# A cross-attention layer and a recurrent layer on one core: the second batch's projections between the first batch's head groups, and nine GpSimd sums a round on VectorE

## The reference

```
scores = einsum('bhqd,bhkd->bhqk', q, k) / sqrt(32)
scores = scores * mask - 10000.0 * (1.0 - mask)
ctx = einsum('bhqk,bhkd->bhqd', softmax(scores), v)
```

```
a = k_t[:, None] * v_t[None, :]
out = einsum('i,ij->j', r_t, u * a + s)
s = a + w_t[:, None] * s
```

## Time and profile before

| | us |
|---|---|
| median of 3 runs (2052.15 to 2056.28) | 2054.96 |
| the profiled execution | 2053.13 |
| its span, first to last instruction | 2051.4 |
| TensorE busy | 1899.5 (93%) |
| VectorE busy | 1445.3 (70%) |
| ScalarE busy | 870.5 (42%) |
| GpSimd busy | 486.0 (24%) |

### The profile page before, as it was taken

One profiled execution on the slowest core, in us unless ns is written; L12 is line 12 of the kernel. 1 busy time (PEld: TensorE's weight loads), 2 busy tenths in 40 slices (PEclk: granted clock), 3 DMA queues, 4 the chain that ended last, 5 costly groups with the idle time before them and its releaser, 6 DMA issues.

```text
span 2051.4 us, 29340 instructions
## 1 busy us (share of the span) xinstructions
PE 1899.5 (93%) x11284; PEld 1293.4 (63%) x11284; DVE 1445.3 (70%) x2472; ACT 870.5 (42%) x2068; POOL 486.0 (24%) x234
## 2 busy tenths in 40 slices
PE   6789999999999999989799999999999999997577
PEld 4566666667666666566576666766767766766343
DVE  3366666767666635236968978888889889789972
ACT  2466666666666656221243243242332431321222
POOL 2233333343433322120221211212202202112000
PEclk9799999999999999999899999999999999999788
DMA  7000000101001021643554464563644644625330
GB/s 216 19 9 27 11 27 12 32 7 36 27 11 47 32 88 42 209 168 113 180 189 157 154 203 141 187 204 126 209 169 162 213 160 138 205 101 166 113 103 31
DMA packets 152788, 227.80 MB, mean 111 GB/s; under 512 B 24185, under 2 KB 72057, under 8 KB 152649
## 3 DMA queue, kind: packets, MB, share of 16 engines
q1 hardware_dynamic: 127272, 205.07, 30.4%
q10 hardware_dynamic: 25376, 20.86, 3.2%
HBM read 183.94 MB, written 41.96 MB: 110 GB/s over the span
## 4 chain that ended last, share of the span: by engine, by line
PE 44%; DVE 6%; DMA 3%; issue 2%; ACT 2%; POOL 1%; ACTq 1%; DVEq 0%; SPq 0%; POOLq 0%
PE b_f_bank L1805 9%; PE b_f_bank L1795 9%; PE b_a_bank L1828 7%; PE b_c_bank L1838 7%; PE b_c_bank L1828 3%; DVE b_ring L2144 2%; PE b_y_bank L1897 2%; PE b_a_bank L1861 2%; DMA b_o<-b_o_all 1%; POOL b_mixed L1714 1%; DVE b_ring L2133 1%; DMA b_o_all<-b_osum 1%; PE b_f_bank L1925 1%; ACTq L2466 1%; PE b_a_bank L1882 1%
## 5 line engine op out<-in xcount | busy, mean ns | idle before, releaser
L406 POOL TENSOR_TENSOR a_prob<-a_prob,a_rowinv 128x1024 f32<-128x1024 f32 x128 | 242.2, 1893 | 504.7 <-DVE a_rowinv L861 504.6
L1093 ACT ACTIVATE a_prob<-a_score,a_low 128x256 f32<-128x256 f32 x512 | 253.6, 497 | 228.1 <-DVE a_low L853 228.1
L2144 DVE TENSOR_TENSOR_SCAN b_ring<-b_ws,b_ring 128x1028 f32<-128x1028 f32 x128 | 312.4, 2482 | 3.6 <-ACT b_ring L2449 0.7
L1795 PE MATMUL b_f_bank<-k_hT_early,k_w_early 128*128 128x256 f32 x896 | 208.9, 388 | 3.9 <-DVE k_enc_early L2248 2.5
L1805 PE MATMUL b_f_bank<-k_w_early 128*128 128x512 f32 x448 | 204.3, 607 | 0.0
L853 DVE CUSTOM_DVE_ANT_0 a_score<-a_score,a_fill 128x256 f32<-128x256 f32 x512 | 196.6, 446 | 4.8 <-DVE a_score L840 0.2
L1795 PEld LDWEIGHTS b_f_bank<-k_hT_early,k_w_early 128*128 128x128 f32 x896 | 169.4, 192 | 40.7 <-issue 18.3
L840 DVE SCALAR_TENSOR_TENSOR a_score<-a_S,a_mask 128x1024 f32<-128x1024 f32 x128 | 150.7, 1219 | 49.5 <-PE a_S L600 49.5
L1714 POOL TENSOR_TENSOR b_mixed<-b_mixed,b_xaT 128x1024 f32<-128x1024 f32 x39 | 114.2, 2945 | 299.9 <-DVE b_mixed L2170 279.6
L2133 DVE TENSOR_TENSOR b_ring<-b_ks,b_vs 128x2048 f32<-128x2048 f32 x64 | 180.4, 2820 | 3.2 <-issue 3.2
L833 DVE TENSOR_SCALAR a_ctxT<-a_O,a_vec 128x256 f32<-128x256 f32 x64 | 31.0, 484 | 207.6 <-PE a_O L630 207.6
(11 more groups left out here) (201 smaller groups left out, 3004.0 us busy)
## 6 DMA issues: line engine op xcount, KB each, us to landing
k_w_early<-in_w_dram SPq DMA_DIRECT2D x64, 1024.0 KB, 5.5
b_vs<-b_v_all SPq DMA_DIRECT2D x32, 512.0 KB, 5.0
b_shared<-in_Wv_dram SPq DMA_DIRECT2D x8, 1024.0 KB, 6.1
b_shared<-in_Wk_dram SPq DMA_DIRECT2D x8, 1024.0 KB, 5.3
b_shared<-in_Wo_dram SPq DMA_DIRECT2D x8, 1024.0 KB, 6.1
b_shared<-in_Wfk_dram SPq DMA_DIRECT2D x8, 1024.0 KB, 7.9
b_shared<-in_Wfv_dram SPq DMA_DIRECT2D x8, 1024.0 KB, 5.3
b_w_all<-b_wT ACTq DMA_DIRECT2D x8, 514.0 KB, 4.4
```

The source lines that it names most:

```text
L406: nc.gpsimd.tensor_tensor(two, two, inv.to_broadcast([P, 2 * TT, SEQ]), ALU.mult)\
L1093: last = nc.scalar.activation(prob[:, slot, a * SEQ:(a + 1) * SEQ], score[:, j, a * SEQ:(a + 1) * SEQ], ACT.Exp, bias=low[:, head, a:a + 1 ...
L1795: last = nc.tensor.matmul(bank[:, m * SEQ:(m + 1) * SEQ], w1[:, cg, col_:col_ + P], hTf[:, cg, :], start=(cg == 0), stop=(cg == CG - 1))
L2144: last = nc.vector.tensor_tensor_scan(x_, flat(ws[:, :, :]), x_, 0.0, ALU.mult, ALU.add)
```

## The change

In the first layer, iteration 0 keeps only its four head groups, and batch 1's transposes, Q, K and V (new stream "pre") stand between them. What slots 4 to 7 did for batch 0 (encoder transposes, output product, second norm's transposes) moves into slots 0 to 3 of iteration 1, with batch 0's cross Q, K and V and batch 2's norm (streams "late_self" and "late_cross"). The new tiles have banks of their own choice (`PRE`, `LATE`). As batch 1's Q and K are made while batch 0's are in use, batch 0's self part uses buffer 0 of Q, K, V and context, all other self parts buffer 1 and cross attention buffer 0 (`home`); batch 0's residual goes to `xo` in place of `xb`. On the DMA queue the vectors ln1_s and ln1_b go first with a semaphore of their own, the encoder rows go behind the biases, and batch 1's x is loaded ahead of the big weights, behind a wait for batch 0's norm and residual. GpSimd makes the residual ahead of the first normalisation.

In the second layer all of GpSimd's sums but the residual with bias are made by VectorE, at places in its order shown below.

```diff
+        PRE = [("pre", "hT1_pre", "act", 2), ("pre", "hT1_pre", "act", 0), ("pre", "q_pre", "dve", 1),
+               ("pre", "k_pre", "act", 2), ("pre", "q_pre", "dve", 0), ("pre", "k_pre", "act", 1),
+               ("pre", "v_pre", "dve", 2), ("pre", "v_pre", "dve", 0)]
+        LATE = [("late_self", "encT_0", "act", 1), ("late_self", "encT_0", "act", 2),
+                ("late_self", "ao_0", "dve", 0), ("late_self", "ao_0", "dve", 1), ("late_cross", "xk_0", "act", 2),
+                ("late_cross", "xk_0", "act", 0), ("late_self", "hT2_0", "act", 2),
+                ("late_self", "hT2_0", "act", 0), ("late_cross", "xv_0", "dve", 1), ("late_cross", "xq_0", "dve", 2),
+                ("late_cross", "xq_0", "dve", 0), ("late_cross", "xv_0", "dve", 2)]
+        def home(at, d):
+            return 0 if at or d == 0 else 1
...
-            iteration(Turn(0, ("self", "next"), ("next",)))
-            iteration(Turn(1, ("cross", "self", "next"), ("self", "next")))
+            iteration(Turn(0, ("pre",), ("pre",)))
+            iteration(Turn(1, ("late_self", "late_cross", "self", "next"), ("pre",)))
...
+            sp.wait_ge(h_made["next"].sem, h_made["next"].at(0, 1))
+            alone(sp)
+            sp.wait_ge(xb_made.sem, xb_made.at(0, 1))
+            alone(sp)
+            load_x(1)
+            load_enc(0)
             for name, tile in (("w_ao", w_ao), ("w_q", w_q), ("w_kv", w_kv), ("w_co", w_co)):
...
                 begin(0)
+                if pre:
+                    fill.hidden_self(1)
+                if late:
+                    pe.wait_ge(weights_in, 16 * N_WEIGHT_DMAS)
+                    fill.encoder(0)
                 turn(0)
+                if pre:
+                    fill.self_q(1, 0)
+                if late:
+                    fill.self_out(0, 0)
                 end(0)
                 begin(1)
+                if pre:
+                    fill.self_k(1, 0)
+                if late:
+                    fill.self_out(0, 1)
                 turn(1)
+                if pre:
+                    fill.self_q(1, 1)
+                if late:
+                    fill.cross_k(0, 0)
+                    fill.cross_k(0, 1)
                 end(1)
                 begin(2)
+                if pre:
+                    fill.self_k(1, 1)
+                if late:
+                    fill.hidden_cross(0)
+                    fill.cross_v(0, 0)
                 turn(2)
+                if pre:
+                    fill.self_v(1, 0)
+                if late:
+                    fill.cross_q(0, 0)
                 end(2)
                 begin(3)
+                if pre:
+                    fill.self_v(1, 1)
+                if late:
+                    fill.cross_q(0, 1)
                 turn(3)
+                if late:
+                    fill.cross_v(0, 1)
+                    fill.hidden_self(2)
                 end(3)
+                if pre:
+                    return
```

The order on VectorE in the second layer:

```diff
                 if a is not None:
+                    nc.vector.tensor_tensor(sx[:, :, :], xaT[:, :, 0:SEQ], xaT[:, :, 1:SEQ + 1], ALU.subtract)\
+                        .then_inc(sx_made.sem, 1)
                     dve.wait_ge(sx_made.sem, sx_made.at(a, 1))
...
                     shift_pair(a, (0, 1), 1)
+                    add_xa(a, 0)
+                    add_xa(a, 1)
...
                     shift_pair(a, (2, 3), 1)
+                    add_xa(a, 2)
+                    add_xa(a, 3)
...
                     for k in range(2):
                         shift(a, 4, k)
-                    if f is None:
-                        dve.wait_ge(*emptied(a, "mix4", 1))
-                        nc.vector.tensor_tensor(mixed[:, 0, :, :], mixed[:, 0, :, :], xaT[:, :, 1:SEQ + 1], ALU.add)\
-                            .then_inc(mix_made.sem, 1)
+                    add_xa(a, 4)
                     dve.wait_ge(*emptied(a, "r", 1))
                     nc.vector.tensor_tensor(mixed[:, 1, :, :], kT[:, :, :], rT[:, :, :], ALU.mult).then_inc(rk_made.sem, 1)
+                    if s is not None and f is not None:
+                        for tally in (bv_in, o_in):
+                            dve.wait_ge(tally.sem, tally.at(s, 1))
+                        nc.vector.tensor_tensor(o[:, :, :], o[:, :, :], bv[:, :, :], ALU.add).then_inc(o_made.sem, 1)
                     step(a, 0)
+                    if s is not None and f is not None:
+                        dve.wait_ge(rstd_made.sem, rstd_made.at(s, 1))
+                        nc.vector.tensor_tensor(o[:, :, :], o[:, :, :], sq[:, :, :], ALU.mult).then_inc(y_made.sem, 1)
...
                 if s is not None and f is not None:
+                    dve.wait_ge(*emptied(s, "xcT", 1))
+                    nc.vector.tensor_tensor(sx2[:, :, :], xcT[:, :, 0:SEQ], xcT[:, :, 1:SEQ + 1], ALU.subtract)\
+                        .then_inc(sx2_made.sem, 1)
                     mix_channel(s)
```

More of the change, by code:

```diff
@@ L918, in iteration @@
                 lows(1)
+                if pre:
+                    take_q(1, "q_pre", 0, "b_q1", 0)
+                if late:
+                    take_self_out(0, 1, False)
+                    ln_var(0, "self")
                 if out:
@@ L927, in iteration @@
                     ln_var(0, "tail")
-                if more:
+                if more and cross:
                     dve.wait_ge(x_in.sem, x_in.at(b + 1, 1))
@@ L933, in iteration @@
                 end(1)
+                if late:
+                    dve.wait_ge(*g_filled(1, "hT1_pre", 1))
+                    ln_apply(0, "self", x)
                 begin(2)
                 lows(2)
+                if pre:
+                    take_q(1, "q_pre", 0, "b_q1", 1)
+                if late:
+                    dve.wait_ge(x_in.sem, x_in.at(2, 1))
+                    for a in range(TT):
+                        ln_half("next", x_new, a)
+                    ln_var(2, "next")
                 if cross:
                     take_q(b - 1, "xq", 1, "b_q", 1)
+                if cross or late:
                     dve.wait_ge(mask_in.sem, mask_in.at(b - 1, 1))
                     fill_mask(1).then_inc(fill_made.sem, 1)
-                if more:
-                    if self_ and cross:
-                        dve.wait_ge(*g_filled(b - 1, "hT2", 1))
+                if more and cross:
+                    dve.wait_ge(*g_filled(b - 1, of_first("hT2", b - 1), 1))
                     ln_apply(b + 1, "next", x_new)
@@ L954, in iteration @@
                 lows(3)
+                if pre:
+                    take_v(1, "v_pre", 0, 0)
+                if late:
+                    dve.wait_ge(*g_filled(0, "hT2_0", 1))
+                    ln_apply(2, "next", x_new)
+                    take_q(0, "xq_0", 1, "b_q", 1)
                 if cross:
@@ L1127, in iteration @@
                 t7, t8 = (st in t.streams for st in ("t7", "t8"))
+                if pre:
+                    hidden_self(1)
                 softmax(0)
+                if late:
+                    encoder(0)
                 softmax(1)
+                if pre:
+                    self_k(1, 0)
+                if late:
+                    root(0, "self")
+                    cross_k(0, 0)
+                    cross_k(0, 1)
+                    hidden_cross(0)
                 if cross:
                     cross_k(b - 1, 0)
-                if more:
+                if more and cross:
                     root(b + 1, "next")
@@ L1138, in iteration @@
                 softmax(2)
+                if pre:
+                    self_k(1, 1)
+                if late:
+                    root(2, "next")
                 if cross:
                     cross_k(b - 1, 1)
-                if more:
+                if more and cross:
                     hidden_self(b + 1)
@@ L1147, in iteration @@
                 softmax(3)
+                if pre:
+                    return
+                if late:
+                    hidden_self(2)
                 softmax(4)
@@ L1188, in _ @@
             self_k(0, 1)
+            root(1, "next")
             run_iterations(act, iteration)
```

286 lines of the change are left out of this document (157 added, 129 removed).

## The result

The changed kernel takes 2031.39 us in the median of four runs (2025.70 to 2034.61) against 2055.62 (2052.15 to 2058.07): ratio 0.9885, 95% interval 0.9871 to 0.9899. The forecast was 2025, range 2010 to 2040. The profiled execution has a span of 2028.7 us where the one before has 2051.4, 22.7 less; the median of the runs is 24.2 less. One run of all those in this document, of the experiment part2, took 3304.31 us at a mean granted clock of 0.555 and is left out of its figures.

The account below looks back on a forecast made before the run. TensorE was taken to set the second layer's rounds (139.58 of 141.56 us busy), with idle time in the first layer's early slots. 2053.1 - 31 (first layer) + 2.4 (second) = 2024.5, stated as 2025; range 2010 to 2040.

Parts of the forecast that it names:

- First layer, the slots: Eight slots of iterations 0 and 1, with projections spread into idle time: 93.2 us instead of 120.2, 27.0 less.
- I take 11.0: Slot 0 of iteration 0, with transposes and one tile: 11.0 us, just above the floor of 10.8.
- First layer, the start: Earlier channel vectors 2.5 us, waits for taking Q and K gone 1.2 each: 4.9 us less.
- VectorE's bill: Second layer: nine sums add 11.0 us a round, GpSimd's exit returns 11.5, VectorE stays at 119 us.
- the scans: Second layer, VectorE: 16 scans a round at 2.53 us, taken as 2.29 undisturbed, each giving back 0.24.
- the extreme case: Shared port lock: each removed GpSimd sum returns its whole 2.2 us, nine give 20, VectorE ends 9 lighter.
- Second layer, the hand-offs: TensorE's waits for o plus bonus, fifth mix sum and gate: a steady round 1.55 us longer, six rounds 8.7.
- the credit of 2.4: Second layer, five places where VectorE's ring steps set the pace: an estimated 0.5 us less at each.
- rival 1: First layer: new slots don't hold the clock or first loads come late, adding about 15 us: 2040; chance 0.15.
- Rival 2: Second layer: GpSimd's exit frees more, rounds fall to TensorE's sum, 21 us less: 2004; chance 0.08.
- Rival 3: Second layer: VectorE becomes the bound, each sum lengthens the round, 11 us x 6: about 2080; chance 0.05.
- Rival 4: First layer: each slot stretches by the projections it takes in, the 27 us almost vanish: about 2052; chance 0.02.

Follow-up runs that it names:

- part2: First layer as in the kernel before, second layer as changed (nine sums on VectorE): 2063.20 us, ratio 1.0031 against the kernel before.
- banks: Changed kernel with other banks for the second batch's tiles in iteration 0 of the first layer: 2029.95 us, ratio 0.9879 against the kernel before.
- part1: First layer as changed, second layer as in the kernel before: 2024.34 us, ratio 0.9854 against the kernel before.
- fifth_mix_only: First layer as changed; against the second layer of before, only the fifth mix sum moved to VectorE in every round: 2014.22 us, ratio 0.9810.
- o_first: Changed kernel with VectorE's o plus bonus ahead of the fifth mix sum and the product of K and R: 2017.42 us, ratio 0.9818 against the kernel before.
- two_on_gpsimd: Changed kernel with o plus bonus and o times the inverse deviation back on GpSimd: 2014.01 us, ratio 0.9802 against the kernel before.
- vectors_late: Changed kernel with the first norm's two channel vectors issued last of ten on the DMA queue: 2037.03 us, ratio 0.9913 against the kernel before.

## Why the prediction was right, and where it was off

**First layer, the slots.** Forecast 93.2 us, found 95.5. Seven of the eight lie within 0.7 us: 11.6, 10.9, 10.5, 11.5, 14.4, 11.8, 11.8 from slot 1 on, against 11.0, 11.0, 10.8, 10.8, 14.6, 12.0, 12.0. The step that was off is the first, "I take 11.0": 13.2. The prediction counted tiles and floor but did not follow the bank of the second half of the transposes. That bank holds a V tile which VectorE takes behind two score masks; ScalarE then takes the transposes late and loads its table behind them. The lines of slot 0 above show it (masks, then the V tile, then transposes and table), and banks by taking the bank away: 10.95. The clock came back as forecast, to 0.96 and 0.97.

**First layer, the start.** Forecast 4.9, found 4.2, in part1 4.7. Its terms: the vectors 2.3 to 2.4 (forecast 2.5), and both bank waits gone. What is missing is a wait of 0.55 us for the next weights, which were late for the earlier tile. The next x came in time: TensorE waited for its norm nowhere. Together the forecast kept 31, and the tile at 162.10 has 28.9. The 27.2 at the second layer's first tile have 1.7 less, by the clock behind the wait of 3.17 us, which the forecast could not know from one trace.

**Second layer, VectorE's bill.** Forecast: 11.0 in, 11.5 back, busy for 119. Found: 119.56 a round. Nine sums gave back 10.4 us (118.99 + 11.0 - 119.56), 1.2 each and not their whole length. The term that was too large is the scans: undisturbed they take 2.41 us in the mean and not 2.29, so 16 of them gave back 2.0 and not 3.8. A length was misread too: the nine sums average 2.7 us on GpSimd in the round before, not 2.2. That GpSimd slows VectorE is plain in the rows, product of K and R 2.75 before and 1.22 after. The Trainium skill ("SBUF — State Buffer", section "SBUF: two separate sides") has the shared port pair locked for the whole of an instruction. The trace agrees as far as it goes: the product lost 1.53 us, less than the 1.9 to 3.3 us of a single sum on GpSimd. What failed is only the extreme case, that every removed sum gives its whole length back.

**Second layer, the hand-offs.** The prediction had TensorE waiting 2.2 us for o plus bonus; it waits 2.13. No wait for a mix sum: so it is. The gate's wait was to come from the exponential and a sum behind it; it is 1.26. A round was to be 1.55 longer; three of the four steady ones are 1.2 to 1.3 longer (+1.30, +1.21, +1.27). The first round was to gain 3.9, its wait: found -3.2 for that stretch. part1 has -0.2 there and fifth_mix_only -3.6, so it is the fifth sum's. But the size is in part luck. The wait of 3.95 us gave way to one of 2.85 for the gate, which the prediction did not count, and 2.6 us came from the gate product, which ran at a clock of 0.72 before and 1.00 after.

**What was missed: +2.4 forecast, +4.5 found.** The sum by its terms: the six rounds were to cost 8.7 and cost 7.6, of which 1.7 are the low clock in the round of 144.46 (last section); the first round was to give 3.9 and gave 3.2; the credit of 2.4 at places where VectorE sets the pace came out as nothing. That last term is the step that was mis-sized, and no run shows the credit. What stands in its place are stretches that vary by themselves: the second layer's first 66 us have -2.1 in the changed kernel and in part1, and the last two stretches +2.1 and +2.8, without any of these sums moved in part1. Against part1 the last two are 0.7 shorter, which is within what such stretches vary by. By the medians (2031.39 against 2024.34) and the ratios the second part costs 6 to 7 us, more than the 2.7 between the profiled runs, since part1's profiled run lies 3.4 above its median and the changed kernel's 1.0 below.

**The total.** The forecast was 2024.5 for a profiled run, and it took 2030.43. The first layer gave 3.8 less than kept and the second took 2.1 more. The step from 2024.5 to 2025 is a slip as well: with the 1.8 that the prediction names, it is 2026.3.

**What the prediction did not ask.** It placed the round's length at the hand-offs, and o_first, two_on_gpsimd and fifth_mix_only confirm that. It did not ask what the second part is worth term by term. It would have found one good one (the fifth sum: 3.4 once and about 1.2 a round), two bad ones at the places they were given and six idle ones.

**Rivals.** The clock held (0.96 and more), so rival 1 has only the late slot 0 in it. Rival 2 is refuted: the rounds grew, and they came near TensorE's sum only where the two bad sums stood elsewhere on VectorE or on GpSimd. Rival 3 (VectorE the bound, 11 us a round) is refuted by the rounds, 1.2 to 1.3 longer, and by o_first. Rival 4: slots did not stretch, all but the first stand within 0.7 us of the forecast.

## What to carry to other kernels

Where a stage leaves TensorE waiting for the other engines, tiles of another batch that need none of its results belong into the gaps: a block of 31 us of TensorE's tiles went into slots that the other engines held open, and the eight slots grew from 89.2 to 95.5 us only. Follow every bank back to the engine that empties it and to what stands ahead on that engine. When sums are moved from one engine to another, sort them by who waits for each: here one of nine brought the whole gain, two lost more than it where they stood, and an operation that a third engine waits for goes ahead of those for which nobody waits.

## What the runs showed of the hardware that was not expected

The wait of 2.13 us for o plus bonus seems to bring down TensorE's clock now and then. The changed kernel's timeline in its long round, and the window of the slow tile:
```profile
1450.10 3.72 PE L1918 MATMUL b_f_bank<-k_hT_early,k_w_early 128*128 128x256 f32 x16
1455.95 3.47 PE L1970 MATMUL b_c_bank<-b_o,k_dev_head 128*128 128x256 f32 x8 [2.13 <-DVE b_o L2493]
1459.21 3.87 PE L1951 MATMUL b_a_bank<-b_mixed,b_Wg 128*128 128x256 f32 x16
```
```profile
1456.00:1459.20 3.20, 3.20 (x8) 2.56 (x9) 3.07 (x2) 0.60 (x1) 0.00 (x0) 0.55 0.55 197
```
The same tile that took 1.99 us in the round before takes 3.47, with the granted clock of its window at 0.55, near the lower of the two levels (1.2 of 2.4 GHz), and the round's TensorE time rises from 139.30 to 141.00. The other slow tiles shown above, behind waits of 3.17 and 2.33 us, are of the same kind. In the five rounds from the second scan on, such a slow stretch at this place stands six times in the 20 rounds of the four kernels that have the wait (once in the changed kernel and in banks, twice in part2 and vectors_late), and never in the 40 rounds of the other eight, the kernel before among them, where TensorE's wait for o is mostly 0 to 0.6 us and in one of part1's rounds 1.9. The first scan round has the wait too, in the same four kernels, and is slow in none. So a wait of 2.1 us can cost 3.8. Another place counts the same way: TensorE's deviation tile in the stretch before the last (1903.81 before) takes 2.85 to 3.78 us in the five traces where it waited 2.33 to 4.65 us for its input, and 1.98 in the seven where it waited 0.83 to 1.96. These are counts over twelve traces; that the wait is the cause is not shown by an experiment that changes it alone, and what decides between the rounds stays open.

The banks and the vectors change single waits of 2 to 2.5 us, and the runs of one kernel lie up to 9 us apart (2025.70 to 2034.61). Such terms were read from the tiles in the traces, not from the medians.
